# Two heads per stack buffer in two row halves, and the two score passes in pairs

## The chip, the cores and the metric

The kernel runs on one core of a Trainium2 chip. The time is that of one launch on the device, in microseconds (us). The engines are TensorE (PE: matmuls; PEld is its weight load), VectorE (DVE), ScalarE (ACT), GpSimd (POOL) and SyncE (SP), which here issues nearly all of the DMAs.

## The reference

Two layers of an adaptively normalised transformer block, each an attention and a mixture of experts, over 32 batches of 256 tokens with 128 features. Cut to what matters here, the attention of layer 0 is

```python
H, Hd = (16, 8)
slopes = jnp.power(2.0, 8.0 * jnp.arange(0, -H, -1, dtype=jnp.float32) / H)
q, k, v = ...                      # from LayerNorm(x) modulated, (B, 16, 256, 8)
scores = jnp.einsum('bhqd,bhkd->bhqk', q, k) / math.sqrt(Hd)
bias = -slopes[:, None, None] * jnp.abs(pos[None, :] - pos[:, None])
probs = jax.nn.softmax(scores + bias[None], axis=-1)
out = jnp.einsum('bhqk,bhkd->bhqd', probs, v)
x = x + ga * (out @ W_out.T + b_out)
```

Layer 1 has the same shapes, no position bias and no output projection. After each attention come a second normalisation and the experts (top 2 of 8 in layer 0, top 1 of 8 in layer 1), whose rows are scattered to HBM by expert, gathered in tiles of 256 and scattered back.

## The kernel before

**Stages.** The program is setup, attention of layer 0, experts of layer 0, attention of layer 1, experts of layer 1. `attention` is written once for both layers; the change lies in it, and in the tables that setup loads.

**Ticks.** Every engine runs its own queue, and `run_ticks` (L377) walks all of them through *ticks*, one per batch. In tick i `at(0)` is batch i, `at(1)` the next, `at(-1)` the one before; a batch is loaded and normalised at +3 and +2, its q and k are projected at +1, its first score pass is at 0, its second pass and the weighing of the values at -1, the rest at -2 and -3. The order inside a tick is written out by hand in a `tick` function per engine, and engines wait for each other by counting semaphores. 6 ticks ahead of and 6 behind the loop are unrolled; between them a hardware loop runs 13 times over two ticks.

**Stack rows.** Scores need more precision than bf16 gives, so q and k (128 rows of head parts, 256 tokens) are split on POOL (`split_qk`, L584, four operations) into three bf16 parts each. For six products of parts, SP's `stack_up` (L514) copies eight rows of each head into the buffer `stack[u]`: head by head along the free axis, the 48 product rows along the partitions, with rows for the position bias (LIN) and for the maxima (MROW, the last two of 128 partitions; those between are zero). One DMA writes 8 partitions by 8 heads by q and k by 256 tokens from 64 partitions of `parts`; a batch takes twelve, six for heads 0 to 7 (issued at `at(1)`) and six for heads 8 to 15 (issued first thing in the batch's own tick). Two buffers alternate.

**Two passes.** `scores_a` (L1114) computes the scores of one head (two matmuls of 256 columns over 126 rows, and in layer 0 two of 128 columns that add the distance term) into PSUM tile A[h % 2]; DVE's `row_max` (L863) takes the row maxima. After eight heads `split_max` (L869) writes the negated maxima in two bf16 parts, PE's `turn_max` (L1130) turns them, ACT's `max_rows` (L709) copies them to `mrow`, and SP's `stack_max` (L524) puts them in the stack as two more rows. One tick later `scores_b` (L1137) computes transposed scores with the maximum already taken off, over all 128 rows, two heads per chunk, into PSUM tile B[c % 2]; ACT's `exps` (L715) exponentiates them to `probs`, and `weigh` (L1153) multiplies four heads with their values as four 32-column tiles of the PE array. `turn_heads` turns the sums back and DVE divides.

**Order on PE** (L1193): sixteen `scores_a` and eight `scores_b` in a fixed pattern, with the small steps between (turning h2, q and k, gate, values, output projection, counting). `turn_max(-1, 1)` stands after head 6 and `turn_max(0, 0)` after head 15. PSUM tile M0 is shared by all small steps, and `m0_read` waits for the reader before. A score matmul of head h waits for the maximum of head h - 2; chunk c waits for the exponentials of chunk c - 2; heads 0 and 8 wait for the stack rows, chunks 0 and 4 for the maxima rows.

**Order on SP** (L549): second half of the stack rows of `at(0)`, maxima of the second half of `at(-1)`, loads, first half of the stack rows of `at(1)`, a store or load, and last the maxima of the first half of `at(0)`. SP is in order: a step that waits holds all behind it.

**Order on POOL** (L636): split, gate values (layer 1), modulate, scatter by four (layer 0) or two (layer 1) indirect DMAs, expert sums (layer 1), wait for the scatter to land.

Of the kernel before, what the change touches and what calls it, by code (L numbers as in the profile page):

```python
# [34 lines left out]
MROW = P - 2  # L35
# [87 lines left out]
def build(nc, a, out):  # L123
    with ExitStack() as ctx:
# [6 lines left out]
        def dram(name, shape, dt=F32):  # L131
# [58 lines left out]
        stack = [sb(f"stack{u}", [P, H, 2, S], BF16) for u in range(2)]  # L190
        vals = [sb(f"vals{u}", [P, NT, H, VW]) for u in range(2)]
        mx = [sb(f"mx{u}", [P, H, NT]) for u in range(2)]
        mneg = sb("mneg", [P, 2, NT, 2, HH], BF16)
# [73 lines left out]
        stack_rows = [(stack[u][first:first + 2, :, :, :], a["stack_rows0"][n:n + 2].bitcast(BF16))  # L267
                      for u in range(2) for n, first in ((0, LIN), (2, MROW))]
        loaded, ready, modp, moded, mod_out = (sem(n) for n in
            ("setup_loaded", "setup_ready", "setup_products", "setup_modulation", "mod_rows_written"))  # L270
        stack_zero, stack_loaded = sem("setup_stack_zeroed"), sem("setup_stack_loaded")
# [3 lines left out]
        with nc.Block() as block:  # L275
            @block.sync
            def _(sp):
                for dst, src in loads:
                    sp.dma_start(dst, src).then_inc(loaded, 16)
                sp.wait_ge(stack_zero, 2)  # L280
# [35 lines left out]
            def _(dve):  # L316
                ch = Chain(dve, set_dve)
                for u in range(2):
                    dve.memset(stack[u][:, :, :, :], 0.0).then_inc(stack_zero, 1)
# [56 lines left out]

def run_ticks(eng, tick, ch=None, per=0):  # L377
# [5 lines left out]

    for i in range(-DEPTH, DEPTH):
        tick(peeled(i))
    pairs = (B - 2 * DEPTH) // 2
    if ch:
        ch.before()
    with eng.Fori(0, pairs) as k:
        if ch:  # L390
            ch.loop(k, 2 * per)
        for i in (DEPTH, DEPTH + 1):
            tick(lambda off: (k * 2 + (i + off), k + (i + off) // 2, (i + off) % 2))
        if ch:
            assert ch.n == 2 * per, ch.n
    if ch:
        ch.done(pairs)
    for i in range(DEPTH + 2 * pairs, B + DEPTH):
        tick(peeled(i))


def attention(nc, l, g):
# [38 lines left out]
    m_in = Transfers([[sem(f"m_in{u}{h}") for h in range(2)] for u in range(2)], 1)  # L441
# [28 lines left out]
    with nc.Block() as block:  # L470

        @block.sync
        def _(sp):
# [1188 lines left out]
```

## Time and profile before

| | |
|---|---|
| median of 3 runs | 2246.19 us (2245.32 to 2248.29) |
| the profiled execution's own time | 2240.77 us |
| its span | 2239.0 us, mean granted TensorE clock 0.943 |
| PE busy | 1779.3 us, 79% |
| DVE busy | 1652.0 us, 74% |
| ACT busy | 1039.1 us, 46% |
| POOL busy | 881.2 us, 39% |
| costliest group | the row maxima on DVE (L867), 1024 of them, 691.8 us, 682 ns each |
| first pass matmuls (L1122) | 2048, 433.2 us busy, 283 ns each with their overlap |
| second pass matmuls (L1146) | 2048, 357.7 us busy, 277 ns each with their overlap |

The span is from the first to the last instruction of one profiled execution. Busy is the union of an engine's instructions; matmuls overlap, so their mean is longer than the distance between their starts. A wait names what ended an idle stretch. In a row of the timeline the columns are start in us, duration in us, engine, line, operation, output <- inputs, shapes and count, and in brackets the idle time before it and what ended that. A clock of 1.00 is 2.4 GHz, 0.50 is 1.2 GHz.

### The profile page before, as it was taken

The numbers are of one execution on the slowest core, as the hardware profiler recorded it, in microseconds if no ns is written. First come the engines' busy times: TensorE is split into PE (matmuls) and PEld (weight loads), VectorE is DVE, ScalarE is ACT, GpSimd is POOL, SyncE is SP. The second block draws the span as 40 slices with busy tenths as digits, with TensorE's granted clock in tenths as the row PEclk, the third lists the DMA queues.
The fourth block names the chain that finished last, engine by engine and source line by source line (L and its number), as shares of the span: only waits on it lengthen the run. The fifth ranks groups of instructions, "written<-read, shape, count | busy, mean of one in ns | idle before, by whom it ended". The sixth has DMA issues, their size and how long they took to land. (4 is left out here: it accounts for less than half of the span.)

```text
span 2239.0 us, 57857 instructions
## 1 busy us (share of the span) xinstructions
PE 1779.3 (79%) x15650; PEld 1283.3 (57%) x15650; DVE 1652.0 (74%) x5861; ACT 1039.1 (46%) x1967; POOL 881.2 (39%) x932
## 2 busy tenths in 40 slices
PE   2599999999999947999935777777777878719997
PEld 1366666666666727999822444444444444417775
DVE  3488888888888855666626899899898888724453
ACT  0266666666666632222212555555555655603322
POOL 0224444444444333444423444444444444203333
PEclk9999999999999978999966999999999998959999
DMA  3343444343444323222235545545555454243332
GB/s 119 50 65 71 71 70 72 71 70 71 72 71 71 67 52 74 68 68 67 65 121 82 100 98 107 102 99 106 101 102 107 97 102 101 59 146 92 96 93 63
DMA packets 266022, 189.09 MB, mean 84 GB/s; under 512 B 25896, under 2 KB 256202, under 8 KB 265246
## 3 DMA queue, kind: packets, MB, share of 16 engines
q1 hardware_dynamic: 250602, 153.34, 34.7%
q0 software_dynamic: 15360, 35.03, 5.4%
q8 instruction: 28, 0.46, 0.1%
q14 instruction: 32, 0.26, 0.1%
HBM read 93.27 MB, written 53.18 MB: 65 GB/s over the span
## 5 line engine op out<-in xcount | busy, mean ns | idle before, releaser
L867 DVE TENSOR_REDUCE mx<-A 128x2 f32<-128x512 f32 x1024 | 691.8, 682 | 132.2 <-PE A L1126 52.8
L720 ACT ACTIVATE probs<-B 128x1024 f32<-128x1024 f32 x512 | 524.5, 1024 | 380.0 <-PE B L1146 195.5
L1122 PE MATMUL A<-stack 126*128 126x256 bf16 x2048 | 433.2, 283 | 136.2 <-DVE mx L867 102.5
L1146 PE MATMUL B<-stack 128*128 128x256 bf16 x2048 | 357.7, 277 | 32.6 <-DMA stack<-mrow 32.4
L1122 PEld LDWEIGHTS A<-stack 126*128 126x128 bf16 x2048 | 182.0, 99 | 296.8 <-DVE mx L867 213.9
L1161 PE MATMUL M<-probs,vals 128*32 128x256 f32 x4096 | 286.7, 396 | 22.0 <-DVE On L893 16.7
L629 POOL DMA_INDIRECT gathered<-h,slot_in x192 | 187.4, 976 | 154.4 <-DVE slot_in L1014 108.8
L1146 PEld LDWEIGHTS B<-stack 128*128 128x128 bf16 x2048 | 197.2, 101 | 84.3 <-issue 30.6
L616 POOL TENSOR_TENSOR h<-xn,back_rows 128x256 f32<-128x256 f32 x64 | 46.4, 726 | 498.9 <-DVE xn L822 498.9
L1562 PE MATMUL A<-w2s,hid 128*128 128x128 f32 x1792 | 230.4, 278 | 9.1 <-issue 9.1
L1562 PEld LDWEIGHTS A<-w2s,hid 128*128 128x128 f32 x1792 | 211.8, 192 | 18.4 <-issue 13.4
L1553 PE MATMUL B<-xtT,w1s 128*128 128x256 f32 x896 | 215.2, 393 | 5.3 <-DVE xtT L1439 2.0
L1368 POOL DMA_INDIRECT expert_out<-yt,row_dest x144 | 138.4, 961 | 175.4 <-DVE yt L1474 141.1
L1126 PE MATMUL A<-dist,slope_ident 128*128 128x128 bf16 x1024 | 200.6, 221 | 0.0
L1553 PEld LDWEIGHTS B<-xtT,w1s 128*128 128x128 f32 x896 | 167.4, 194 | 39.8 <-issue 16.4
L1161 PEld LDWEIGHTS M<-probs,vals 128*32 128x32 f32 x4096 | 124.9, 111 | 103.9 <-issue 33.9
L1149 PE MATMUL B<-dist,slope_ident 128*128 128x128 bf16 x1024 | 183.5, 219 | 0.0
L1522 ACT ACTIVATE hid<-B 128x1024 f32<-128x1024 f32 x72 | 73.8, 1024 | 226.6 <-PE B L1553 226.6
L592 POOL TENSOR_TENSOR parts<-qk,ones_col 128x512 bf16<-128x512 f32 x64 | 66.5, 1039 | 256.2 <-ACT qk L698 116.4
L1365 POOL DMA_INDIRECT out<-yt,row_dest x80 | 84.6, 1058 | 170.5 <-DVE yt L1479 147.0
L727 ACT ACTIVATE heads<-M 128x256 f32<-128x256 f32 x256 | 98.2, 384 | 106.3 <-PE M L1161 105.8
L1526 ACT ACTIVATE hid<-B,b 128x256 f32<-128x256 f32 x160 | 62.8, 475 | 174.0 <-PE B L1553 138.0
(192 smaller groups left out, 2980.0 us busy)
## 6 DMA issues: line engine op xcount, KB each, us to landing
stack<-parts SPq DMA_DIRECT2D x768, 64.0 KB
xt<-gathered SPq DMA_DIRECT2D x112, 132.0 KB, 2.2
probs<-gathered SPq DMA_DIRECT2D x40, 256.0 KB, 2.7
w<-in_w SPq DMA_DIRECT2D x4, 2048.0 KB
back_rows<-mod_rows SPq DMA_DIRECT2D x64, 128.0 KB, 3.3
x_mid<-X SPq DMA_DIRECT2D x64, 128.0 KB, 1.9
Y<-expert_out SPq DMA_DIRECT2D x64, 128.0 KB
X<-in_x SPq DMA_DIRECT2D x32, 128.0 KB, 3.0
```

Of the source, the lines that this page charges most:

```text
L629: pool.indirect_dma_start(gathered[l], bass.IndirectOffsetOnAxis(ap=slot_in[u][:, c, t:t + 1], axis=0), (h3 if l else h2)[u][:, t, :], Non ...
L720: act.activation(probs[c % 4][:, :, :, :], Bp[c % 2][:, :, :, :], ACT.Exp, scale=EXP_SCALE[l][c // 4]).then_inc(b_exp.handle, 1)
L727: act.activation(heads[g % 2][:, :], M1[:, 0:S], ACT.Copy).then_inc(o_read.handle, 1)
L867: dve.tensor_reduce(mx[u][:, h, :], A[h % 2][:, :, :], AX.X, ALU.max).then_inc(a_max.handle, 1)
L1122: ins = pe.matmul(A[h % 2][:, t, :], stack[u][0:n, h, 0, t * P:(t + 1) * P], stack[u][0:n, h, 1, :], start=True, stop=(l == 1))
L1126: ins = pe.matmul(A[h % 2][:, t, t * P:(t + 1) * P], slope_ident[:, h % HH, :], dist[:, t, :], start=False, stop=True)
L1146: ins = pe.matmul(Bp[c % 2][:, j, t, :], stack[u][:, h, 1, t * P:(t + 1) * P], stack[u][:, h, 0, :], start=True, stop=(l == 1))
L1149: ins = pe.matmul(Bp[c % 2][:, j, t, t * P:(t + 1) * P], slope_ident[:, h % HH, :], dist[:, 1 - t, :], start=False, stop=True)
L1161: ins = pe.matmul(M1[VW * j:VW * j + VW, 0:S], vals[u][:, t, 4 * g + j, :], probs[(2 * g + j // 2) % 4][:, j % 2, t, :], start=(t == 0), s ...
L1368: ins = pool.indirect_dma_start(expert_out[l], dest, yt[u][:, t, :], None)
L1553: ins = pe.matmul(dst[:, f, :], w1s[u][:, f * P:(f + 1) * P], xtT[u][:, :], start=True, stop=True)
L1562: ins = pe.matmul(A[u][:, t, 0:D], hid[u][:, f, t * P:(t + 1) * P], w2s[u][:, f, :], start=(f == 0), stop=(l == 0 and f == FC - 1))
```

## The change

The stack buffer holds two heads in one column: even heads in partitions 0 to 63, odd heads in 64 to 127, each with its 48 product rows, two position rows and two maxima rows (52 in use; the zero rows and their memsets go). Buffers become half as long, and four of them rotate instead of two. `stack_up` issues all twelve DMAs of a batch at `at(1)`; `stack_max` issues two DMAs instead of one. First and second pass matmuls are issued in pairs by `scores`: pair n holds the first pass of head n of `at(0)` in one row half and the second pass of one head of `at(-1)` in the other. PE turns the maxima earlier (after pair 1 and pair 10), and ACT's `max_rows` move with it. The loops run over four ticks six times instead of two ticks thirteen times, only on their own engine, with an aligned start and a hint for the back edge. Weights' columns are permuted to match.

```diff
-MROW = P - 2
+MROW = LIN + 2
+ROWS = MROW + 2
+HALF = P // 2
+STACKS = 4
...
-        stack = [sb(f"stack{u}", [P, H, 2, S], BF16) for u in range(2)]
+        stack = [sb(f"stack{v}", [P, HH, 2, S], BF16) for v in range(STACKS)]
...
+def loop_of(eng, rounds):
+    return eng.bass.Fori(0, rounds, engines=bass.OrderedEngineSet([eng.engine]), head_slot={eng.engine: 0},
+                         hint_back_edge=True)
...
-    pairs = (B - 2 * DEPTH) // 2
+    rounds = (B - 2 * DEPTH) // STACKS
...
-            def stack_up(b, k, u, half):
-                if half == 0:
-                    sp.wait_ge(split.handle, split.after(b))
-                sp.wait_ge(b_scores.handle, b_scores.after(b - 2, 4 * half + 4))
-                for r, (pq, pk) in enumerate(PRODUCTS):
-                    src = parts[u][:, :, :, :].rearrange("p q r s -> p (q r) s")
-                    sp.dma_start(stack[u][HD * r:HD * r + HD, HH * half:HH * half + HH, :, :],
-                                 src[64 * half:64 * half + 64, pq:4 + pk:3 + pk - pq, :])\
-                        .then_inc(stack_in[u][half], 16)
+            def stack_up(b, k, u, v):
+                sp.wait_ge(split.handle, split.after(b))
+                if not isinstance(b, int) or b >= STACKS:
+                    sp.wait_ge(b_scores.handle, b_scores.after(b - STACKS, HH))
+                for j in range(2):
+                    for r, (pq, pk) in enumerate(PRODUCTS):
+                        src = parts[u][:, :, :, :].rearrange("p q r s -> p (q r) s")
+                        first = HALF * j + HD * r
+                        sp.dma_start(stack[v][first:first + HD, :, :, :],
+                                     src[HALF * j:HALF * j + HALF, pq:4 + pk:3 + pk - pq, :])\
+                            .then_inc(stack_in[u][j], 16)
...
+            def stack_max(b, k, u, v, half):
                 sp.wait_ge(mT_read.handle, mT_read.after(b, half + 1))
-                sp.dma_start(stack[u][MROW:MROW + 2, HH * half:HH * half + HH, 0, :], mrow[half][:, :])\
-                    .then_inc(m_in[u][half], 16)
+                for j in range(2):
+                    first = HALF * j + MROW
+                    sp.dma_start(stack[v][first:first + 2, 4 * half:4 * half + 4, 0, :], mrow[half][8 * j:8 * j + 8, :])\
+                        .then_inc(m_in[u][half], 16)
...
-            def tick(at):                                  # SP
-                if at(0):
-                    stack_up(*at(0), 1)
+            def tick(at, slot):
                 if at(-1):
-                    stack_max(*at(-1), 1)
+                    stack_max(*at(-1), slot(-1), 1)
...
                 if at(1):
-                    stack_up(*at(1), 0)
+                    stack_up(*at(1), slot(1))
                 if at(-2):
                     (load_gate if l else store_x1)(*at(-2))
...
                 if at(0):
-                    stack_max(*at(0), 0)
+                    stack_max(*at(0), slot(0), 0)
...
+            def scores(at, slot, n):                       # PE
+                c, j = n // 2, n % 2
+                if at(0):
+                    b, k, u = at(0)
+                    if n < 2:
+                        pe.wait_ge(stack_in[u][j], stack_in.of(k))
+                    pe.wait_ge(a_max.handle, a_max.after(b, n - 1) if n >= 2 else a_max.after(b - 1, H + n - 1))
+                if at(-1) and j == 0:
+                    b, k, u = at(-1)
+                    if c % 4 == 0:
+                        pe.wait_ge(m_in[u][c // 4], m_in.of(k))
+                    pe.wait_ge(b_exp.handle, b_exp.after(b, c - 1) if c >= 2 else b_exp.after(b - 1, HH + c - 1))
+                for t in range(NT):
+                    if at(0):
+                        rows = stack[slot(0)][HALF * j:HALF * j + MROW, c, :, :]
+                        last_a = pe.matmul(A[j][:, t, :], rows[:, 0, t * P:(t + 1) * P], rows[:, 1, :], ...)
+                    if at(-1):
+                        rows = stack[slot(-1)][HALF * (1 - j):HALF * (1 - j) + ROWS, c, :, :]
+                        last_b = pe.matmul(Bp[c % 2][:, 1 - j, t, :], rows[:, 1, t * P:(t + 1) * P], rows[:, 0, :], ...)
+                if l == 0:
+                    # the distance matmuls over 128 rows: two of A, then two of B
...
+                pair(0)
+                pair(1)
+                if at(-1):
+                    turn_max(*at(-1), 1)
+                pair(2)
                 heads_step(weigh, -2, 3)
                 if at(-3):
                     turn_h2(*at(-3))
+                pair(3)
                 if at(1):
                     project_qk(*at(1))
...
+                pair(10)
+                if at(0):
+                    turn_max(*at(0), 0)
                 heads_step(weigh, -1, 1)
+                pair(11)
...
+                pair(15)
                 if at(2):
+                    m0_read((pos_read, -3), ...)
                     turn(by_tile(xn[at(2)[2]]), xn_ready, at(2)[0], xn_T)
```

Setup issues eight loads of four stack rows each instead of four of two, and layer 1 reloads its two position rows by eight DMAs instead of two.

## Rows read from the trace of the kernel before

**Rows 1.** The page, part 6: the DMA issues that fill the stack.

```profile
stack<-parts SPq DMA_DIRECT2D x768, 64.0 KB
```

**Rows 2.** Windows: us, busy (count) of PE, PEld, DVE, ACT, POOL, clock, DMA.

```profile
550.00:600.00 50.00, 46.93 (x520) 34.68 (x519) 43.45 (x145) 30.80 (x58) 21.60 (x23) 1.00 0.40 68
1550.00:1600.00 50.00, 38.94 (x348) 23.84 (x348) 44.97 (x153) 29.70 (x62) 23.74 (x27) 0.97 0.47 98
```

**Rows 3.** Waits, 200 to 750 us: total us, times, longest.

```profile
DVE mx L867 <- PE A L1126: 28.9, 48, 0.6
```

**Rows 4.** Waits, 1300 to 1850 us.

```profile
DVE mx L867 <- PE A L1122: 29.1, 46, 0.9
```

**Rows 5.** Timeline of POOL in layer 0: last split of one batch, split of the next.

```profile
398.97 1.19 POOL L595 TENSOR_TENSOR parts<-rem,parts 128x512 bf16<-128x512 f32 x1
...
418.50 1.04 POOL L592 TENSOR_TENSOR parts<-qk,ones_col 128x512 bf16<-128x512 f32 x1 [2.91 <-DMA gathered<-h,slot_in]
...
421.99 1.15 POOL L595 TENSOR_TENSOR parts<-rem,parts 128x512 bf16<-128x512 f32 x1
```

**Rows 6.** Timeline of SP in layer 0: stack rows of the next batch.

```profile
400.27 3.99 SPq L520 DMA_DIRECT2D stack<-parts  x6
```

**Rows 7.** Timeline of PE in layer 0: first matmul of two ticks.

```profile
408.92 0.28 PE L1122 MATMUL A<-stack 126*128 126x256 bf16 x1 [0.27 <-DMA stack<-parts]
...
453.87 0.28 PE L1122 MATMUL A<-stack 126*128 126x256 bf16 x1 [0.24 <-DMA stack<-parts]
```

**Rows 8.** Windows of the second tick of layer 0, columns as in rows 2.

```profile
90.00:102.00 12.00, 5.72 (x38) 4.11 (x39) 4.88 (x13) 2.18 (x5) 0.00 (x0) 0.63 0.58 66
102.50:106.00 3.50, 3.50 (x35) 2.84 (x36) 2.02 (x6) 2.30 (x4) 0.70 (x1) 0.89 0.00 0
```

**Rows 9.** Timeline of SP and PE there.

```profile
89.08 3.95 SPq L520 DMA_DIRECT2D stack<-parts  x6
93.07 0.69 SPq L526 DMA_DIRECT2D stack<-mrow  x1
...
97.95 0.40 PE L1122 MATMUL A<-stack 126*128 126x256 bf16 x1 [5.57 <-DMA stack<-parts]
...
110.00 4.05 SPq L520 DMA_DIRECT2D stack<-parts  x6
```

**Rows 10.** Window behind the 5.57 us of idle, columns as in rows 2.

```profile
97.50:103.00 5.50, 5.05 (x32) 4.08 (x33) 3.54 (x10) 1.41 (x3) 0.00 (x0) 0.50 0.51 54
```

**Rows 11.** Timeline of PE and SP over one tick of layer 1.

```profile
1494.41 0.61 PE L1122 MATMUL A<-stack 126*128 126x256 bf16 x4
...
1506.43 4.01 SPq L520 DMA_DIRECT2D stack<-parts  x6
...
1517.57 0.69 SPq L526 DMA_DIRECT2D stack<-mrow  x1
...
1518.20 0.60 PE L1122 MATMUL A<-stack 126*128 126x256 bf16 x4
1519.70 0.61 PE L1146 MATMUL B<-stack 128*128 128x256 bf16 x4 [0.90 <-DMA stack<-mrow]
```

**Rows 12.** Timeline of SP and PE in the fill of layer 1.

```profile
1203.49 3.96 SPq L520 DMA_DIRECT2D stack<-parts  x6
...
1210.57 0.71 SPq L526 DMA_DIRECT2D stack<-mrow  x1
...
1214.72 1.03 PE L1146 MATMUL B<-stack 128*128 128x256 bf16 x4 [1.46 <-DMA stack<-mrow]
```

**Rows 13.** Timeline of PE in layer 0: two score matmul pairs, then the weighing.

```profile
410.92 0.22 PE L1126 MATMUL A<-dist,slope_ident 128*128 128x128 bf16 x1
410.98 0.27 PE L1122 MATMUL A<-stack 126*128 126x256 bf16 x1
411.09 0.22 PE L1126 MATMUL A<-dist,slope_ident 128*128 128x128 bf16 x1
411.24 1.07 PE L1161 MATMUL M<-probs,vals 128*32 128x256 f32 x16
```

More of the change, by code:

```diff
@@ L266, in build @@
         ]
-        stack_rows = [(stack[u][first:first + 2, :, :, :], a["stack_rows0"][n:n + 2].bitcast(BF16))
-                      for u in range(2) for n, first in ((0, LIN), (2, MROW))]
+        stack_rows = [(stack[v][HALF * j + LIN:HALF * j + ROWS, :, :, :], a["stack_rows0"][j].bitcast(BF16))
+                      for v in range(STACKS) for j in range(2)]
         loaded, ready, modp, moded, mod_out = (sem(n) for n in
             ("setup_loaded", "setup_ready", "setup_products", "setup_modulation", "mod_rows_written"))
-        stack_zero, stack_loaded = sem("setup_stack_zeroed"), sem("setup_stack_loaded")
+        stack_loaded = sem("setup_stack_loaded")
         gates_out = sem("gate_rows_written")
@@ L382, in peeled, with slot @@
         return lambda off: (i + off, (i + off) // 2, (i + off) % 2) if 0 <= i + off < B else None
+    def slot(i):
+        return lambda off: (i + off) % STACKS
     for i in range(-DEPTH, DEPTH):
-        tick(peeled(i))
-    pairs = (B - 2 * DEPTH) // 2
+        tick(peeled(i), slot(i))
+    rounds = (B - 2 * DEPTH) // STACKS
     if ch:
         ch.before()
-    with eng.Fori(0, pairs) as k:
+    with loop_of(eng, rounds) as k:
         if ch:
-            ch.loop(k, 2 * per)
-        for i in (DEPTH, DEPTH + 1):
-            tick(lambda off: (k * 2 + (i + off), k + (i + off) // 2, (i + off) % 2))
+            ch.loop(k, STACKS * per)
+        for i in range(DEPTH, DEPTH + STACKS):
+            tick(lambda off: (k * STACKS + (i + off), k * (STACKS // 2) + (i + off) // 2, (i + off) % 2), slot(i))
         if ch:
-            assert ch.n == 2 * per, ch.n
+            assert ch.n == STACKS * per, ch.n
     if ch:
-        ch.done(pairs)
-    for i in range(DEPTH + 2 * pairs, B + DEPTH):
-        tick(peeled(i))
+        ch.done(rounds)
+    for i in range(DEPTH + STACKS * rounds, B + DEPTH):
+        tick(peeled(i), slot(i))
 def attention(nc, l, g):
@@ L440, in attention @@
     stack_in = Transfers([[sem(f"stack_in{u}{h}") for h in range(2)] for u in range(2)], len(PRODUCTS))
-    m_in = Transfers([[sem(f"m_in{u}{h}") for h in range(2)] for u in range(2)], 1)
+    m_in = Transfers([[sem(f"m_in{u}{h}") for h in range(2)] for u in range(2)], 2)
     x1_out = transfers("x1_out", 1)
@@ L765, in tick @@
                 chunk(0)
+                step(max_rows, -1, 1)
                 step(head_sums, -2, 3)
@@ L780, in tick @@
                 layer(0, read_y, -2)
+                step(max_rows, 0, 0)
                 step(head_sums, -1, 1)
@@ L788, in tick @@
                 step(head_sums, -1, 2)
-                step(max_rows, 0, 0)
                 chunk(7)
@@ L1191, in count, with tick, pair @@
                     .then_inc(pos.handle, 1)
-            def tick(at):
-                def a_pass(*hs):
-                    if at(0):
-                        for h in hs:
-                            scores_a(*at(0), h)
+            def tick(at, slot):
+                def pair(n):
+                    if at(0) or at(-1):
+                        scores(at, slot, n)
                 def m0_read(*uses):
@@ L1634, in inputs_of @@
         "qk_bias": np.stack([bqkv[0:D][stacked], bqkv[D:2 * D][stacked]], 1),
-        "q_scale": np.stack([np.where(np.arange(D) < 64, HD ** -0.5, (2.0 / HD) ** 0.5), np.full(D, D ** -0.5)], 1).astype(f),
+        "q_scale": np.stack([np.where(in_first, HD ** -0.5, (2.0 / HD) ** 0.5), np.full(D, D ** -0.5)], 1).astype(f),
         "vo_bias": np.stack([bqkv[2 * D:][by_head], n["L0_attn_b_out"]], 1),
```

138 lines of the change are left out of this document (55 added, 83 removed).

## The prediction

> **What bounds the kernel now.** I read the page first, for the stages: some 720 us of the 2239.0 us span are the attention of layer 0, some 760 us that of layer 1, the rest is experts and setup, which the change leaves alone but for a few loads. Then the windows: in layer 0 PE is busy 94% and DVE 87% of a stretch, in layer 1 PE 78% and DVE 90% [rows 2]. By shares one would say PE in the first and DVE in the second. The waits say how much each takes from the other: DVE waits for scores 28.9 us in 550 us of layer 0 and 29.1 us in 550 us of layer 1 [rows 3, 4]. A tick (one batch) lasts 22.5 us in layer 0 (first score matmul at 408.92 and, two ticks on, 453.87) and 23.8 us in layer 1 (1494.41 to 1518.20) [rows 7, 11], so these waits are 1.2 us of every tick. That is all that a faster PE can give DVE.
>
> Then the timelines, for what sets the moment at which a tick starts; call it T. In layer 0 the next batch's parts are split on POOL, SP issues six DMAs for the first eight heads, and the first matmul needs them. The split ends at 400.16, SP begins at 400.27, the matmul starts at 408.92, 8.7 us after the split, and its wait is put down to that DMA [rows 5 to 7]. In that tick the next split ends at 423.14 [rows 5], T+14.2, and 8.7 us later is 431.86, 22.9 us after T. So **layer 0 already starts its ticks when the stack rows land**. The split itself starts late, at 418.50 [rows 5], since POOL first modulates and scatters the rows of two earlier batches. In layer 1 the six DMAs start at 1506.43, T+12.0, and 11.8 us are left before the next tick [rows 11]; they are not what is waited for there. What is waited for, 0.90 us before the first second pass chunk, is the DMA with the row maxima, issued at 1517.57, landed by 1519.70 [rows 11].
>
> How fast the stack DMAs go shows best while the pipeline fills: SP issues six from 89.08, a maxima DMA at 93.07, and six more; DMA is busy 0.58 from 90 to 102 and 0.00 from 102.5 on [rows 8, 9]. Twelve DMAs of 64 KB [rows 1] take 12 us of data, 1.0 us each, 1.2 us after the first issue, though SP issues one every 0.66 us (3.99 us for six [rows 6]). It is the transfer, not the issue, that sets their rate, and a small transfer behind them waits its turn: the maxima of 1210.57, issued behind six stack DMAs and the loads of layer 1, are used at 1214.72, 4.2 us later [rows 12], against the 2.1 us of [rows 11].
>
> The Trainium skill ("DMA: Bandwidth & Descriptors", section on why a DMA increments its semaphore by 16) says that a copy runs on as many engines as divide both outer sizes, the lowest-numbered ones: 8 for 8 rows from 64, 2 for the maxima, on the same low engines. That agrees with a busy share near a half and with maxima that queue behind; nothing in the sum is taken from it.
>
> **The change part by part.**
> Stack rows. Before, a batch's twelve DMAs went in two halves, six before its tick and six inside it, the second half being needed only at head 8. Now `stack_up` issues all twelve in one go behind the split, and the second one of the sixteen pairs needs the last of them, since even heads lie in one row half and odd heads in the other. The number and shape of the DMAs stay (8 rows of 4096 elements from 64 rows). Four buffers remove the wait for the second pass two batches ago, which no row shows as late; they do not let the upload start sooner, as it still follows the split of the same tick. From the end of the split: 0.1 to the first issue, 1.2 to the first data, 12.0 of data, 0.9 to the matmul (408.92 less 0.1, 1.2 and six DMAs with a store beside them) = 14.2 us where six took 8.7.
>
> Maxima. PE turns them and ACT reads them earlier (after pairs 1 and 10 instead of heads 6 and 15), which takes the last cause of the 0.9 us in layer 1 away. But on SP `stack_max` of the first half is still the tick's last step, behind twelve stack issues (7.9 us), and now two DMAs. In layer 0 it is issued 8.8 us after the split, behind 12 us of data and the 128 KB store, which I put at 0.5: it lands at 0.1+1.2+12.0+0.5+0.1+0.9 = 14.8 us after the split. In layer 1 seven loads stand before it too. [rows 12] have this case with six stack DMAs: first issue 1203.49, maxima used at 1214.72, 11.2 us; six more stack DMAs add 6.0 and the gate load, absent there, 0.5: 17.7 us. And the new `scores` waits for these maxima in pair 0, ahead of the first pass matmul too. **So T of the next tick is not before the split plus 14.8 us (layer 0) or 17.7 us (layer 1).** Behind the wait stand all of PE's work, DVE's maxima and ACT's exponentials: there is one PE queue.
>
> Split. It can't be earlier than the batch's q and k, projected after pair 3. In the fill, with no scatter in the way, T=97.95 and SP starts at 110.00: 12.05 us, at a granted clock of 0.50 until 103 [rows 9, 10]; weigh, 1.0 us [rows 13], and turning h2, 0.3, come on top in full ticks: 13.3. At the full clock I take off the 2.0 us that the slow 4 us cost: 11.3, below the 12.0 of layer 1 [rows 11]. PE now idles several us in each tick, and after the 5.57 us of idle before 97.95 it ran at 1.2 GHz for 5 us [rows 9, 10]; I take 12.6. The POOL route (scatter first) is no later: its start hangs on the tick before and gets slack as ticks grow.
>
> PE itself. A pair had four matmuls of 256 columns at 0.11 and, in layer 0, four of 128 at 0.06 [rows 13]: 0.66 us, 0.44 in layer 1. Concurrent halves would need two slots of 0.11 for four. Going into and out of the column-tiled weigh costs 0.15 where 0.06 is the spacing [rows 13], 0.09 a switch. A pair in layer 0 switches twice: 0.22+0.22+0.18 = 0.62. Layer 1: 0.22+0.18 = 0.40, 0.22 where two pairs adjoin. PE gains 0.6 to 2 us a tick; no row shows row halves side by side, so the bound is from 0 (or -2.9 if nothing runs together and every switch is paid) to +3.5. It all lies before the new wait and is worth nothing while that wait is last. The Trainium skill ("TensorEngine Tiling (Array Packing)", key properties) says that a change of tiling mode drains the engine, which speaks against switching twice a pair; the 0.09 agrees and is what I used.
>
> Loops, setup. Six back edges for thirteen: at most 0.3 us each on PE (the wait at 408.92 is 0.27 [rows 7]), 4 us in all, hidden by the same wait. Setup loses two memsets beside loads and gains four small DMAs; layer 1 gains six before its first loads, +2 us.
>
> **Sum.** Layer 0: 12.6+14.8 = 27.4 us a tick instead of 22.5, layer 1: 12.6+17.7 = 30.3 instead of 23.8. Over 31 intervals each: 31x4.9 + 31x6.5 = 353 us, +2. The profiled execution took 2240.8 us (span 2239.0), so 2596; the median of the runs lies 5.4 above it: **2600 us**.
>
> **Rivals.**
> A, the rows and maxima are in time and PE's gain counts: half of DVE's 1.2 us a tick goes, 62x0.6 = 38 us, 2208 us. For it: the waits of [rows 3, 4] and PE's share in layer 0. Against it: it decides only where T to split plus twelve landings fit in a tick, 11.3+14.2 = 25.5 against 22.5 and 23.8.
> B, slower, but the small maxima DMAs pass the queue and land 2.1 us after issue (as in [rows 11], where nothing was ahead): then only the odd rows count, needed one pair (0.6) after T: 11.3+13.6 = 24.9 in layer 0; in layer 1 the maxima are issued 13.6 after the split, +2.1, so 27.0: 31x(2.4+3.2) = 174, 2420 us. Against it: [rows 12].
> C, worse: scatter and loads share the engines with the longer burst (+0.8 in layer 0, +1.3 in layer 1) and PE is slow at the start of every tick (13.5): 29.1 and 32.5, 31x(6.6+8.7) = 474, 2720 us. For it: clock 0.50 in [rows 10].
>
> **Chances.** Forecast 0.58, B 0.15, C 0.13, A 0.12, nothing measurable 0.02. A measurement of this kernel can tell 0.2% from no change. Faster 0.12, same 0.02, slower 0.86. The range 2390 to 2710 holds the forecast, B and half of C; A and the rest, 0.2, are left out. By the slower cases alone it is the same range.
>
> **What would show it.** In the profile after: PE's first matmul of pair 0 waits 4 us or more in each tick, for DMA stack<-mrow (forecast) or, in pair 1, stack<-parts (B); SP shows twelve stack issues in a row and the maxima behind them; DVE, PE and ACT are all less busy in the two attentions, the granted clock falls, and the experts' windows are as before. If ticks are under 23 us, the DMA step is wrong; if SP starts its uploads before T+10, the split step is; if the twelve land in under 10 us, the rate of 1.0 us is.

## The result, and the profile after

The changed kernel took 2695.2 us (2693.7 to 2696.2, 4 runs), the kernel before 2247.2 us beside it: ratio 1.200, interval 1.198 to 1.202. The forecast was 2600 us, the range 2390 to 2710. The profiled execution has a span of 2691.9 us, 452.9 more than before.

Where the 452.9 us are: the first split to the last takes 898 us in layer 0 (before 690) and 943 us in layer 1 (before 726), so 425 of them lie in the 62 intervals between ticks. From the last split of layer 0 to the first of layer 1 it is 442 us (425), behind the last split 345 us (333), and ahead of the first one 1 us less than before. The page, part 1 (busy time, share of the span, instructions), and its costliest groups:

```profile
PE 1856.1 (69%) x15650; PEld 1091.8 (41%) x15650; DVE 1667.6 (62%) x5859; ACT 1043.9 (39%) x1967; POOL 879.1 (33%) x932
...
L880 DVE TENSOR_REDUCE mx<-A 128x2 f32<-128x512 f32 x1024 | 697.2, 685 | 504.3 <-PE A L1145 267.2
L1145 PE MATMUL A<-stack 50*128 50x256 bf16 x2048 | 459.3, 318 | 488.3 <-DMA stack<-mrow 332.3
```

The same two groups on the page of the kernel before:

```profile
L867 DVE TENSOR_REDUCE mx<-A 128x2 f32<-128x512 f32 x1024 | 691.8, 682 | 132.2 <-PE A L1126 52.8
L1122 PE MATMUL A<-stack 126*128 126x256 bf16 x2048 | 433.2, 283 | 136.2 <-DVE mx L867 102.5
```

DVE works nearly as long as before (1667.6 us against 1652.0) and waits more: 504.3 us ahead of the row maxima, before 132.2. PE's idle time ahead of the first pass is 488.3 us (before 136.2), and 332.3 of it is put down to one small transfer, the maxima. The windows that answer to [rows 2], one per layer:

```profile
550.00:600.00 50.00, 37.81 (x410) 20.15 (x408) 37.80 (x123) 25.58 (x46) 16.07 (x17) 0.93 0.39 57
1850.00:1900.00 50.00, 36.62 (x294) 16.61 (x294) 36.88 (x124) 24.61 (x49) 18.04 (x20) 0.71 0.36 68
```

Both engines fall to about 75%, and the clock of layer 1 to 0.71. The waits of 200 to 750 us, and of 1500 to 2050 us, where [rows 3, 4] had only DVE's (total us, times, longest):

```profile
PE A L1145 <- DMA stack<-mrow: 91.7, 19, 5.2
DVE mx L880 <- PE A L1154: 109.4, 75, 4.1
...
PE A L1145 <- DMA stack<-mrow: 101.8, 18, 6.9
DVE mx L880 <- PE A L1145: 150.7, 55, 6.8
```

PE has one such wait per tick, of 4.8 us in layer 0 and 5.7 us in layer 1 in the mean. A tick of layer 0 in the timelines of POOL, SP and PE (answers to [rows 5 to 7]):

```profile
408.75 1.18 POOL L608 TENSOR_TENSOR parts<-rem,parts 128x512 bf16<-128x512 f32 x1
410.06 8.03 SPq L531 DMA_DIRECT2D stack<-parts  x12
418.37 0.41 SPq L549 DMA_DIRECT2D x_mid<-X  x1
418.93 11.94 SPq L539 DMA_DIRECT2D stack<-mrow  x4
426.03 0.39 PE L1145 MATMUL A<-stack 50*128 50x256 bf16 x1 [5.20 <-DMA stack<-mrow]
438.32 1.18 POOL L608 TENSOR_TENSOR parts<-rem,parts 128x512 bf16<-128x512 f32 x1
```

The split ends at 409.93, twelve stack issues go out in a row, a store, and the maxima; PE starts 16.1 us after the split, and the next split ends at 439.50, T+13.5. Over the 26 splits between 170 and 920 us the means are 15.9 and 13.4 us. The windows (columns as in [rows 2]) show when the data flow, and the clock at the start of the tick:

```profile
412.00:419.00 7.00, 5.53 (x76) 3.11 (x79) 6.01 (x25) 4.41 (x9) 0.00 (x0) 1.00 0.60 64
...
423.00:424.00 1.00, 0.00 (x0) 0.00 (x0) 0.03 (x1) 0.00 (x0) 0.84 (x2) 1.00 0.58 60
424.00:425.00 1.00, 0.00 (x0) 0.00 (x0) 0.00 (x0) 0.00 (x0) 0.78 (x1) 1.00 0.27 49
...
426.03:431.50 5.47, 5.47 (x43) 2.17 (x43) 3.05 (x9) 1.28 (x2) 1.94 (x3) 0.50 0.11 38
```

The DMA share is about 0.6 from 411.2 to 424.3, 13.1 us for the twelve and the store. In layer 1 (answer to [rows 11]) four ticks in a row (splits 1646.70 to 1740.01) have the split end at T+11.7 to T+12.6 and the next tick start 17.3 to 19.7 us after it; over the 24 splits between 1500 and 2240 us it is 16.4 to 19.9, in the mean 18.7. One of the four, PE, POOL and SP:

```profile
1634.06 0.39 PE L1145 MATMUL A<-stack 50*128 50x256 bf16 x1 [3.34 <-DMA stack<-mrow]
1645.54 1.16 POOL L608 TENSOR_TENSOR parts<-rem,parts 128x512 bf16<-128x512 f32 x1
1659.04 11.03 SPq L539 DMA_DIRECT2D stack<-mrow  x4
1666.39 0.39 PE L1145 MATMUL A<-stack 50*128 50x256 bf16 x1 [6.86 <-DMA stack<-mrow]
```

The pairs do run side by side. In layer 1, at full clock, first and second pass start together, 0.12 us apart, and a pair takes 0.32 us (1615.30 to 1615.62) where four in a row took 0.44:

```profile
1615.30 0.28 PE L1145 MATMUL A<-stack 50*128 50x256 bf16 x1
1615.30 0.28 PE L1149 MATMUL B<-stack 52*128 52x256 bf16 x1
1615.42 0.27 PE L1145 MATMUL A<-stack 50*128 50x256 bf16 x1
1615.42 0.27 PE L1149 MATMUL B<-stack 52*128 52x256 bf16 x1
1615.62 0.48 PE L1126 MATMUL M<-wv_ga,hT 128*128 128x256 f32 x1
```

### The profile page after: what moved, and what is told of

It reads as the page before. It is cut to its first block and busy times, and to the rows that moved or that the text cites. A ratio compares the mean times of both kernels' runs of the same rounds, so it can differ in the third digit from the quotient of the medians.

```text
span 2691.9 us, 57302 instructions
## 1 busy us (share of the span) xinstructions
PE 1856.1 (69%) x15650; PEld 1091.8 (41%) x15650; DVE 1667.6 (62%) x5859; ACT 1043.9 (39%) x1967; POOL 879.1 (33%) x932
## 5 line engine op out<-in xcount | busy, mean ns | idle before, releaser
L880 DVE TENSOR_REDUCE mx<-A 128x2 f32<-128x512 f32 x1024 | 697.2, 685 | 504.3 <-PE A L1145 267.2
L1145 PE MATMUL A<-stack 50*128 50x256 bf16 x2048 | 459.3, 318 | 488.3 <-DMA stack<-mrow 332.3
L1149 PE MATMUL B<-stack 52*128 52x256 bf16 x2048 | 454.1, 317 | 0.0
L1145 PEld LDWEIGHTS A<-stack 50*128 50x128 bf16 x2048 | 129.1, 101 | 758.0 <-issue 538.1
L1180 PE MATMUL M<-probs,vals 128*32 128x256 f32 x4096 | 362.7, 484 | 26.3 <-DVE On L908 23.6
L1180 PEld LDWEIGHTS M<-probs,vals 128*32 128x32 f32 x4096 | 135.1, 129 | 140.9 <-issue 81.2
L1154 PE MATMUL A<-dist,slope_ident 128*128 128x128 bf16 x1024 | 158.6, 241 | 0.0
L1158 PE MATMUL B<-dist,slope_ident 128*128 128x128 bf16 x1024 | 155.4, 238 | 0.0
L1149 PEld LDWEIGHTS B<-stack 52*128 52x128 bf16 x2048 | 128.7, 101 | 13.9 <-issue 6.4
```

Of the source, the lines that this page charges most:

```text
L880: dve.tensor_reduce(mx[u][:, h // HH, :, h % 2, h % HH // 2], A[h % 2][:, :, :], AX.X, ALU.max)\
L1145: last_a = pe.matmul(A[j][:, t, :], rows[:, 0, t * P:(t + 1) * P], rows[:, 1, :], start=(t == 0), stop=(l == 1), skip_group_check=True)
L1149: last_b = pe.matmul(Bp[c % 2][:, 1 - j, t, :], rows[:, 1, t * P:(t + 1) * P], rows[:, 0, :], start=(t == 0), stop=(l == 1), skip_group_ch ...
L1154: last_a = pe.matmul(A[j][:, t, t * P:(t + 1) * P], slope_ident[:, n % HH, :], dist[:, t, :], start=False, stop=True, skip_group_check=True)
L1158: last_b = pe.matmul(Bp[c % 2][:, 1 - j, t, t * P:(t + 1) * P], slope_ident[:, (n + 1 - 2 * j) % HH, :], dist[:, 1 - t, :], start=False, s ...
L1180: ins = pe.matmul(M1[VW * j:VW * j + VW, 0:S], vals[u][:, t, 4 * g + j, :], probs[(2 * g + j // 2) % 4][:, j % 2, t, :], start=(t == 0), s ...
```

## The experiments

They ran in three jobs (sets of kernels run together), A, B and C, each on another chip. In A and B the kernel before took 2375.7 and 2376.4 us, in C 2243.7 us. So ratios hold within a job. Across jobs I compare the mean tick: twenty ticks in the middle of a layer, from starts of POOL's first split operation (405.27 and 434.85 are two such starts of the changed kernel). Other choices of twenty move most values by 0.1 or 0.2, layer 0 of unpair between 33.7 and 35.4. In layer 1 the kernel before has the same tick, 23.8 to 23.9, in the profiles of all jobs (in A and C in those of its variants). The clock does not hold across jobs that well: it was 0.97 in layer 1 of the kernel before at first and 0.93 in B.

| kernel | job | ratio to before (interval) | tick, layer 0 | tick, layer 1 | clock, 1600 to 1900 us |
|---|---|---|---|---|---|
| before | first | | 22.5 | 23.8 | 0.97 (1300 to 1600) |
| changed | first | 1.200 (1.198 to 1.202) | 29.3 | 30.7 | 0.71 |
| before_again | B | | 26.8 | 23.9 | 0.93 (1420 to 1720) |
| after_again | B | 1.139 (1.136 to 1.141) | 29.3 | 30.6 | 0.70 |
| max_act | A | 1.073 (1.071 to 1.076) | 27.5 | 27.1 | 0.76 |
| three_products | A | 1.093 (1.091 to 1.096) | 30.8 | 27.6 | 0.53 |
| col_halves | A | 1.105 (1.102 to 1.107) | 29.7 | 29.1 | 0.69 |
| loops | A | 1.001 (1.000 to 1.003) | 27.1 | 23.9 | 0.94 (1430 to 1730) |
| early_qk | B | 1.067 (1.064 to 1.069) | 27.3 | 27.6 | 0.70 |
| early_max_act | B | 1.057 (1.053 to 1.060) | 27.7 | 26.4 | 0.74 |
| unpair | C | 1.222 (1.214 to 1.229) | 34.5 | 26.1 | 0.74 (1700 to 2000) |
| pad64 | C | 1.060 (1.056 to 1.064) | 23.4 | 25.9 | 0.80 |
| early_max | C | 1.008 (1.006 to 1.010) | 23.2 | 23.9 | 0.96 (1320 to 1620) |
| early_max_halves | C | 1.053 (1.051 to 1.055) | 28.1 | 23.9 | 0.96 (1430 to 1730) |

**Maxima past SyncE's queue** (max_act). Edit of the changed kernel; SyncE's two `stack_max` steps go:

```diff
                 act.activation(mrow[half][:, :], ...).then_inc(mT_read.handle, 1)
+                act.wait_ge(mT_read.handle, mT_read.after(b, half + 1))
+                for j in range(2):
+                    first = HALF * j + MROW
+                    act.dma_start(stack[v][first:first + 2, 4 * half:4 * half + 4, 0, :], mrow[half][8 * j:8 * j + 8, :])\
+                        .then_inc(m_in[u][half], 16)
```

> The changed kernel, but ScalarE issues the two maxima DMAs of each half itself, right after it has copied the maxima, on its own queue; SyncE issues none. In the changed kernel the first matmul of a tick starts 16.1 us (layer 0) and 16.6 us (layer 1) behind the split. Theory (the twelve stack DMAs take 12 us of data and the maxima queue behind them): what is left is the landing of the last stack DMA, 14.2 us behind the split, so a tick shortens by 1.9 us in layer 0 and 2.4 us in layer 1, and the time falls by 31x4.3 = 130 us, to about 2560. Rival (the maxima DMAs alone are slow, the rows land early): T to T goes down to the split plus 9 to 10 us and the time falls by 370 us, to about 2320. Rival (engines, not the issuing queue, make the maxima wait): the tick stays within 0.5 us, 2680 to 2695.

2549.2 us, against 2704.3 for the changed kernel in job B, where the kernel before took as long as in A: 155 us less. PE's wait changes its cause (PE of max_act in layer 0, layer 1):

```profile
435.64 0.28 PE L1146 MATMUL A<-stack 50*128 50x256 bf16 x1 [2.70 <-DMA stack<-parts]
...
1641.18 0.39 PE L1146 MATMUL A<-stack 50*128 50x256 bf16 x1 [3.06 <-DMA stack<-parts]
```

The split before it ends at 420.87 and 1625.10: the rows alone take 14.8 us in layer 0 (forecast 14.2) and 16.1 in layer 1. Ticks fall by 1.8 and 3.6 us (forecast 1.9 and 2.4). The theory holds in layer 0 and is short in layer 1; the maxima behind twelve stack issues are what comes last, and the rows come 1.3 us ahead of them in layer 0 and some 2.6 us in layer 1.

**Half the stack DMAs** (three_products). `PRODUCTS = [(0, 0), (0, 1), (1, 0)]`, which leaves three products of parts out of the scores.

> The changed kernel with three of the six products of parts left out (the low part of q and of k plays no role), so six stack DMAs a batch instead of twelve, all else as it is; matmuls have the same number of columns. Theory (1.0 us of data for each DMA, on the path in every tick): a tick loses 6.0 us in layer 0 and 6.0 us in layer 1 but not below what PE and DVE need, about 22 and 23 us: 29.1 to 23.1 and 30.6 to 24.6, together 31x12.0 = 372 us, to about 2320. Rival (SyncE's issue of 0.66 us sets the rate): 4.0 us a tick and layer, 2450. Rival (something else than the upload is late): under 100 us less.

2596.9 us, 107 us less than the changed kernel in B instead of 372. No DMA is waited for in 1500 to 2200 us of layer 1, yet the tick falls by 3.1 us only, not 6.0. What is late instead is PE at its low clock, in a window of layer 1:

```profile
1600.00:1900.00 300.00, 267.42 (x1737) 115.20 (x1737) 222.88 (x792) 151.89 (x301) 115.04 (x129) 0.53 0.35 74
```

PE is busy 89% and the granted clock is 0.53, close to the 1.2 GHz level throughout. Neither the theory nor a rival had this. Layer 0, with ticks of 30.8 us, can't be read: ScalarE has the stand-still described under the repeated runs (4.6 us in most ticks of 300 to 750 us), and the clock there is 0.77 besides.

**Stack DMAs cut in two** (col_halves). Twelve DMAs of four columns (32 KB) at `at(1)`, twelve as the tick's first step, order of the weights' columns permuted to fit:

```diff
-                        sp.dma_start(stack[v][first:first + HD, :, :, :],
-                                     src[HALF * j:HALF * j + HALF, pq:4 + pk:3 + pk - pq, :])\
+                        first, row = HALF * j + HD * r, HALF * half + 32 * j
+                        sp.dma_start(stack[v][first:first + HD, 4 * half:4 * half + 4, :, :],
+                                     src[row:row + 32, pq:4 + pk:3 + pk - pq, :])\
```

> The changed kernel with its row halves, pairs, early maxima and loops, but each stack DMA is cut into two of four columns (32 KB): twelve for heads 0 to 7 at at(1) behind the split, twelve for heads 8 to 15 as the tick's first step of SyncE, as in the kernel before; the first pass waits for the second set at pair 8 only. Theory (bytes set the rate of the data): twelve of 0.5 us each are then bound by SyncE's issue, 12x0.66 = 7.9, and land about 10.0 us behind the split; maxima follow at 11.5; a tick is 12.6+11.5 = 24.1 in layer 0 and 26 in layer 1 (seven loads more before the maxima), time about 2250+31x(1.6+2.2) = 2370. Rival (a fixed cost for each DMA, whatever its bytes): the twelve still take 12 us, and there are twenty-four a tick: 29 us a tick or more, 2695 or above.

2625.1 us, between the two expectations. Layer 0 has the stand-still of job A and can't be read. In layer 1 the data are quick now; windows of layer 1 in the middle of twelve stack issues, first col_halves, then the changed kernel:

```profile
1712.00:1722.00 10.00, 7.34 (x65) 2.87 (x65) 9.36 (x41) 4.11 (x11) 1.45 (x2) 0.63 0.16 46
```

```profile
1710.00:1720.00 10.00, 6.94 (x61) 2.92 (x61) 9.41 (x39) 3.97 (x8) 1.54 (x3) 0.60 0.55 64
```

DMA share 0.16 instead of 0.55 for 46 instead of 64 GB/s, so the transfer hardly queues any more. Still PE waits for the maxima, because SyncE reaches them last (SP and PE of col_halves, `...` for seven loads):

```profile
1710.57 8.79 SPq L532 DMA_DIRECT2D stack<-parts  x12
...
1723.38 1.35 SPq L540 DMA_DIRECT2D stack<-mrow  x2
...
1727.44 0.39 PE L1148 MATMUL A<-stack 50*128 50x256 bf16 x1 [3.86 <-DMA stack<-mrow]
```

From the split (1710.47) it is 12.9 us to the maxima's issue and 17.0 to PE. So in layer 1 most of the delay is SyncE's order of issues; data that queue come on top only by what the landing takes over 4.1 us, up to 3.3 (1659.04 to 1666.39 above is 7.35).

**Loops alone** (loops). `run_ticks` of the change (four ticks, six rounds, own engine, hint) in the kernel before.

> The kernel before with one part of the change alone: the loops over four ticks six times, each engine its own, aligned start, hinted back edge. Theory: a back edge costs at most 0.3 us on PE and in layer 0 the stack rows are waited for anyway; seven back edges less in each layer: 0 to 4 us faster, 2243 to 2247. Rival (the hinted loops are what cost time in the changed kernel, by fetching): slower by 10 us or more.

Ratio 1.0014 (0.9999 to 1.0029): no gain and no loss that can be told, so the loops are not what costs time in the changed kernel.

**Both kernels again.** Without an edit.

> The changed kernel once more, without an edit, in one job with the next three: in the job before this one the kernel before took 2375.7 us where it took 2247.2 beside the changed kernel's first run, and the others of this job are to be read against both kernels of their own job. Expected if the machine is as at first: ratio 1.20 and layer 0 ticks of 29.1 us; if it is as in the last job, where layer 0 of the kernel before with new loops had ticks of 27.7 us instead of 22.5: 2700 to 2850 us, ratio 1.13 to 1.20.

> The kernel before, without an edit, for its profile in the same job as the next ones. Expected: ticks of 22.5 us in layer 0 if its time is near 2247 us, and of about 27.7 us, with ScalarE and VectorE idle some 3 us in each tick while the scatter's DMAs run, if it is near 2376 us.

The changed kernel: 2704.3 us, 0.3% more than at first, with the same ticks. The kernel before: 2366 us in its one run, ticks of 26.8 us in layer 0. Its waits in 300 to 750 us show what the first profile has not at all:

```profile
ACT heads L727 <- remote: 57.7, 17, 4.9
DVE mx L867 <- remote: 55.6, 16, 3.7
```

ScalarE and VectorE stand 3.4 us in every tick while POOL's four scatter DMAs run, though PE's matmuls that they wait for are recorded as long done. Why it is so in two jobs and not in two others isn't settled. The changed kernel shows no such wait: its scatter runs while PE stands for the maxima anyway (its four DMAs are issued from 423.77 to 428.58, around the tick's start at 426.03). So 1.139 and 1.200 are the same time of the changed kernel against two of the kernel before, which differ in layer 0.

**The split moved up** (early_qk, and early_max_act with the maxima on ScalarE's queue besides). PE and ScalarE of the changed kernel, and POOL of layer 0 (with `DEPTH = 4`; layer 1 keeps its scatter where it was):

```diff
                 pair(0)
+                if at(1):
+                    project_qk(*at(1))
                 pair(1)
...
+                step(read_qk, 1)
                 chunk(0)
...
-                if at(-3):
-                    scatter(*at(-3))
+                if at(-4) and l == 0:
+                    scatter(*at(-4))
+                    scatter_done(*at(-4))
```

> The changed kernel, with the split moved up: q and k are projected after pair 0 instead of pair 3 and read by ScalarE ahead of chunk 0, and in layer 0 POOL scatters after the split, one tick later (DEPTH 4, so that this tick exists). Uploads and maxima stay on SyncE as they are. The split should end some 7 to 8 us after the tick's start instead of 13.5 (layer 0) and 8 to 9 instead of 11.5 (layer 1). Theory (the tick is T to split plus the landing of twelve DMAs and of the maxima): 7.5+16.1 = 23.6 in layer 0 and 8.7+16.6 = 25.3 in layer 1, but the first half's maxima are turned after pair 10, about 16 us into the tick, and stand last on SyncE. 31x(5.5+5.3) = 335 us less than the changed kernel, ratio to before about 1.05. Rival (the upload is not what sets the tick): no less than 1.17.

> The same with the maxima DMAs issued by ScalarE, too. Theory: rows land 7.5+14.2 = 21.7 (layer 0) and 8.7+14.2 = 22.9 us (layer 1) after the tick's start, just below the 22.5 and 23.8 us of the kernel before; what PE and DVE need sets the tick again, and the gain of the pairs (0.6 to 2 us of PE in a tick) shows for the first time: ratio to before 0.98 to 1.01. Rival (the pairs bring PE and DVE nothing, and PE at its low clock after waits costs): 1.02 or more.

Ratios 1.067 and 1.057. The first misses its 1.05: in layer 1 the tick falls by 3.1 us, not 5.3, with the maxima still last on SyncE and waited for in half of the ticks. The second has what the change needs: in 1500 to 2050 us PE waits for a DMA 4 times, 2.0 us in all. Its tick of layer 1 is still 26.4 us, not 23.8 or less: the theory that the pairs' gain would then show falls, and the rival's 1.02 or more is what came. Layer 0 can't be read in this job (27.7 us with the stand-still), but in the next.

**Not in pairs** (unpair). As early_max_act; `scores` issues the first pass of a head alone, and the second pass of two heads after every second head, each with its own wait.

> The kernel of the last job with the split moved up and the maxima on ScalarE's queue (ratio 1.057; in layer 1 a tick of 26.7 us with only 0.1 us a tick of waits for DMAs, PE and VectorE waiting for each other), with one edit: the matmuls are no longer in pairs. First pass of head n, then after every second head the second pass of two heads, each behind its own wait, so no two row halves run at the same time; layout, uploads and loops stay. Theory (what is left over the kernel before is the coupling of the two passes in one pair, which must wait for VectorE and ScalarE both): layer 1 back to about 24 us a tick, 31x2.5 = 80 us less, ratio about 1.02. Rival (the low granted clock, 0.75 in layer 1, makes PE late, and it stems from matmuls in 50 of 128 rows): PE has more to do here, ticks of 26 to 28 us, ratio 1.05 to 1.09.

Layer 1: 26.1 us, as good as in pairs (26.4) and within the rival's 26 to 28. The coupling of the two passes is not what is left. The ratio, 1.222, was in neither expectation: layer 0 goes to 34.5 us a tick, with PE busy 98% of 300 to 750 us at a mean clock of 0.72. A window there:

```profile
501.00:514.00 13.00, 13.00 (x74) 5.08 (x76) 4.64 (x13) 4.48 (x8) 7.61 (x8) 0.50 0.38 64
```

PE is never idle in these 13 us and has 1.2 GHz in all of them.

**Row halves filled up** (pad64). As early_max_act:

```diff
-MROW = LIN + 2
-ROWS = MROW + 2
+MROW = HALF - 2
+ROWS = HALF
```

> The kernel of the last job with the split moved up and the maxima on ScalarE's queue (ratio 1.057, granted clock 0.75 in 600 us of layer 1), with one edit: each row half is filled up, the maxima rows at 62 and 63 and zero rows between, so a first pass matmul runs over 62 rows and a second pass one over 64 instead of 50 and 52; their columns and number stay. Theory (waits alone set the clock): nothing moves, ratio 1.05 to 1.06, clock 0.75 within 0.02. Rival (rows in use count for the clock, as hinted by the run with three products, 26 rows: clock 0.55 at PE 87% busy): clock up to 0.80 or more in layer 1 and 20 us or more gained.

2376.1 us. Windows of early_max_act and of pad64 in layer 1:

```profile
1600.00:1900.00 300.00, 229.72 (x1817) 103.70 (x1813) 229.27 (x841) 156.96 (x320) 122.19 (x139) 0.74 0.59 94
```

```profile
1600.00:1900.00 300.00, 219.75 (x1850) 101.16 (x1844) 237.73 (x860) 158.33 (x323) 122.40 (x138) 0.80 0.59 96
```

The clock is higher, as the rival has it, but the tick gains 0.5 us, 14 us in 31 ticks, less than its 20. The two windows are from different jobs: the kernel before and its variant early_max differ by 0.03 between the same two jobs (0.93 and 0.96), so up to half of the 0.06 may not be the edit's. Layer 0, in a job without the stand-still, has ticks of 23.4 us at clock 1.00 (300 to 750 us) with no DMA waited for: 0.9 us above the kernel before.

**Maxima mid-tick alone** (early_max, and early_max_halves with the scatter split). The kernel before, with

```diff
                 chunk(0)
+                if at(-1):
+                    turn_max(*at(-1), 1)
...
                 heads_step(weigh, -1, 1)
+                if at(0):
+                    turn_max(*at(0), 0)
```

and the old places gone.

> The kernel before with one part of the change alone: PE turns the second half's maxima after chunk 0 instead of after head 6 and the first half's after head 10 instead of head 15, ScalarE and SyncE follow. Theory: the 0.90 us wait for the maxima DMA at the start of a tick of layer 1 goes, VectorE waits 0.5 us less in each: 31x0.5 = 15 us, ratio 0.990 to 0.998. Rival (turning waits for the reader of the shared PSUM tile, VectorE's base in layer 1, 1.3 to 1.5 us in the changed kernel): as much is lost again, ratio 0.998 to 1.01.

> The same, and in layer 0 POOL issues two of a batch's four scatter DMAs behind modulate and the other two behind the split of the next tick, instead of four in a row. In the last two jobs ScalarE and VectorE stood idle 2.5 to 3.4 us in every tick of layer 0 of the kernel before while the four scatter DMAs ran (tick 26.9 us, against 22.5 in the first profile). Theory (four in a row are what makes them stand): ticks of layer 0 of 23 to 24 us, 31x3 = 93 us less, ratio about 0.95. Rival (any scatter DMA does it): two shorter stalls, ratio 0.99 to 1.01. If the kernel before is near 2247 us in this job, no stalls are seen and the ratio is that of the run before.

early_max is 0.8% slower, where the theory had it faster and the rival up to 1.01. The wait for the maxima DMA in layer 1 is gone, and the tick stays: it was no part of what DVE lacked. In layer 0 the tick grows from 22.5 to 23.2 us, since the output's second turn now waits for ScalarE's copy of the maxima and the stack rows come later (waits of PE in 300 to 750 us):

```profile
PE M L1092 <- ACT mrow L713: 12.6, 19, 0.7
PE A L1122 <- DMA stack<-parts: 11.6, 20, 1.0
```

early_max_halves, 1.053, didn't test what it was for: the job had no stand-still to remove. It brought a new wait, in every other tick of layer 0 (DVE, 300 to 750 us), and none in layer 1:

```profile
DVE mneg L877 <- issue: 33.1, 8, 4.3
DVE mneg L878 <- issue: 29.1, 8, 3.7
```

## Why the prediction was right, and where its numbers were off

**The wait.** The mechanism is as written: pair 0 waits for `stack<-mrow` in every tick, SP shows twelve issues in a row with the maxima behind, PE, DVE and ACT are less busy in both attentions, and the clock falls. The wait is not 4 us or more in each tick, as the list of signs had it: every fourth tick of layer 1 waits 3.2 to 4.0 us, and two of layer 0 wait 2.6 and 3.5. A is refuted by every tick, and B too: the maxima are used 4.1 to 7.6 us after issue, not 2.1, and pair 0 waits for them, not pair 1 for the rows.

**The size.** Of this the forecast had less. The measured 2695 us lie nearer to C's 2720 than to the 2600, and 15 us inside the range. C, which had a chance of 0.13, is right in layer 0 (29.1 a tick against 29.3, with 13.5 and 15.6 us for its two steps against 13.4 and 15.9) and not in layer 1 (32.5 against 30.7). C's reason for its second step, scatter and loads beside the burst, was not tried. So the wait was foreseen, and of the sum both steps of layer 0, the second step of layer 1 and the time outside the ticks were put too small.

**Split to tick, layer 0.** Forecast 14.8, measured 16.1 in the tick shown and 15.9 in the mean. In the tick shown the twelve and the store take 13.1 us of data instead of 12.5 (the first data at 411.2), and from their end to the matmul it is 1.7 us, not 1.0. Two maxima DMAs stand there now; that they take the 0.7 us was not tried.

**T to split, layer 0.** Forecast 12.6, measured 13.5, C's value. The first 5.5 us behind T have a clock of 0.50 in three of four ticks in a row (starts 367.99, 426.03 and 455.38) and 0.60 in the other (396.95). The fill had the same 0.50 for 5 us [rows 10], of which the sum counted 4; of the 2.0 us that these cost I had taken 0.7 off 13.3, and nothing was to be taken off.

**Layer 1.** T to split 12.0 (forecast 12.6), split to tick 18.7 in the mean (17.7), tick 30.7 (30.3). That the sum comes out within 0.4 us is partly luck: one step is 0.6 too long, the other 1.0 too short, and the make-up of the second is partly wrong: [rows 12] gave me 17.7 with a queue of data in it, and col_halves has 17.0 without one. SyncE's twelve issues and seven loads ahead of the maxima are the larger part.

**Pairs.** The 0.09 us for a switch held (0.20 between the last stack matmul and the first distance matmul of a pair, where the spacing is 0.12, so 0.08), and the pair is cheaper than I put it: 0.55 us in layer 0 (404.78 to 405.33) and 0.32 in layer 1, against 0.62 and 0.40. It was worth nothing, as forecast. What I had not seen is that it stays so when the wait that hides it is gone: rival A's gain of 38 us isn't there in any run. With rows and maxima in time, or nearly, the ticks are 23.4 and 25.9 us (pad64), slower than before by 0.9 and 2.1.

**Outside the ticks.** Forecast 2 us, measured 28. Most of it is the emptying of the pipeline, which the sum had as unchanged: from the last split to the first matmul of the experts it is 111 us instead of 97 in layer 0 and 117 instead of 104 in layer 1, 26 us together. Of these, 8 and 9 lie ahead of the last score matmul, in ticks that the 31 intervals between splits don't count; 6 more in layer 0 are a longer wait for the gathered rows (34.9 us instead of 28.9), whose cause was not looked for. The experts of layer 0 themselves are almost as before, 279 us instead of 278 from their first such matmul to their last, with a clock of 0.96 (1060 to 1350 us) where it was 0.99 (850 to 1140).

**The sum.** From the first split to the last, layer 0 grows by 208 us where 31x4.9 = 152 were forecast, layer 1 by 217 where 31x6.5 = 202 were, and outside it is 28 instead of 2. That is 98 us too little, the distance of the profiled execution (2693.7) from the 2596 forecast for it; the medians, 2695 against 2600, are 95 apart.

**What each part costs**, in layer 1, from the table and in the order in which the parts were taken away, partly across jobs: maxima last on SyncE 3.6 us a tick (30.7 to 27.1), the late rows 0.7 (27.1 to 26.4), 50 instead of 62 rows of the array in use 0.5 (26.4 to 25.9), and 2.1 us (25.9 to 23.8) for what is left of the change and of my edits. Of these 2.1 a lower clock, 0.80 against 0.96 (early_max in the same job), and an order in which PE waits for VectorE's base and norm at turns are in the profile; how they share it isn't settled, and that the clock follows from rows in use is suggested by three runs, not shown by them. In layer 0 the maxima cost 1.8 (29.3 to 27.5), the late rows and the rows in use together 4.1 (27.5 to 23.4), and 0.9 are left.

No version beat the kernel before, and none with the new stack layout came within 5% of it.

## What to carry to other kernels

When two halves of an upload are merged so that the first work needs the last byte, add up issue, data and everything behind them on the same queue, the smallest transfer too: here two DMAs of 4 KB, the maxima of half a batch, ended 332 us of PE's idle time. A cheaper matmul is worth nothing while something else sets the moment at which its tick may start. That its gain would show once that wait is gone is a claim of its own, to be measured with the wait taken away: here it did not show. And a step moved earlier that shares a PSUM tile with others can be a new wait for those behind it, as in early_max (22.5 to 23.2 us a tick in layer 0).

## What the runs showed of the hardware that was not expected

**A busy PE at the low clock.** Fewer rows of the array went with a lower clock in layer 1: 26 rows in use per half 0.53 (three_products, job A, PE busy 89%), 50 rows 0.74 (early_max_act, B, 77%), 62 rows 0.80 (pad64, C, 73%), and 126 rows in one piece 0.97 (before, 77%). The jobs alone make 0.04 of difference (0.97 at first, 0.93 in B, for the kernel before), so the ends of this row are clear and the step from 50 to 62 rows less so. unpair's 13 us without any idle time ran at 0.50. The Trainium skill ("TensorE: Matmul & The Clock Gate", Part 1) has the clock follow how busy the engine has been of late; busy time as this profile counts it does not tell the clock here.

**Small stack DMAs are cheaper than their bytes.** 32 KB ones moved 46 GB/s at a DMA share of 0.16, 64 KB ones 64 GB/s at 0.55. The small ones also read 32 source partitions instead of 64, and which of the two differences does it was not tried. SyncE's issue (8.79 us for twelve) is then what sets the rate.

**A wait of 3.4 us on VectorE at the back edge of its loop, in some kernels and in layer 0 only.** Timeline of DVE in the changed kernel, two of these waits:

```profile
280.90 0.20 DVE L889 TENSOR_SCALAR mneg<-mx 128x16 bf16<-128x16 f32 x1 [3.35 <-issue]
...
397.15 0.17 DVE L889 TENSOR_SCALAR mneg<-mx 128x16 bf16<-128x16 f32 x1 [3.41 <-issue]
```

They are 116.3 us apart, one round of the loop, and stand before the first instruction of VectorE's tick. I had put back edges at 0.3 us, from PE alone. Here PE's wait hides it. In early_max_halves, whose loop has two ticks, two waits of 3.5 to 4.3 us in a row come with every other tick, which takes 33 us instead of 23.3. But a back edge alone doesn't bring the wait: layer 1 of both kernels runs through the same kind of loop without it, and so does layer 0 of loops and early_max, apart from 2.8 us where the loop of loops is entered (138.91 us). The Trainium skill ("Runtime: NRT & Kernel Launch", Instruction fetch mechanics) says that a taken branch whose target isn't loaded must fetch it first; the place agrees, but what decides whether the wait appears was not found, and that the fetch is slower beside other DMAs was not tried.
